# Convolutional attention block on one core: pairs 0 and 1 normalised each by itself, statistics of four pairs on ScalarE, pair 0's bias added behind its products

## The chip, the core and the metric

One NeuronCore of a Trainium2 chip runs the kernel alone. The metric is the device time of one execution in microseconds (us). All times are us unless marked ns. Engines: TensorE (PE), VectorE (DVE), ScalarE (ACT), GpSimd (POOL), and SyncE (SP), which issues transfers.

## What is computed

The input is 16 images of 64 channels and 16 x 16 pixels, all float32. The reference, cut to its core (`_gn` has 32 groups, that is two channels each, and so has the first `group_norm`; the second has one group):

```python
h = _gn(x)
xn = group_norm(h, gn1_w, gn1_b, 32)
qkv = einsum('oc,bchw->bohw', qkv_w, xn) + qkv_b
q, k, v = split(qkv, 3)               # 8 heads of 16, n = 256 pixels
q_norm = softmax(q * scale, axis=-1)  # over pixels
k_norm = softmax(k, axis=-2)          # over the 16 of a head
context = einsum('bhdn,bhen->bhde', k_norm, v)
out = einsum('bhde,bhdn->bhen', context, q_norm)
out = einsum('oc,bchw->bohw', out_w, out) + out_b
out = group_norm(out, gn2_w, gn2_b, 1)
return x + out + h
```

## The kernel before

Two images, a "pair", fill the 128 partitions (2 x 64 channels), so there are 8 pairs, 0 to 7. x is loaded by SyncE in four transfers: pair 0, pair 1, pairs 2 and 3, (then the weights), pairs 4 to 7. The two normalisations of x are folded into one affine, `xn = coef_a * x + coef_b`, per channel and pair.

The program is written out engine by engine; each engine runs its instructions in program order, and semaphores tie the engines together. Nothing is scheduled by a tool: the order around the change is the order of the calls at the end of each engine's block.

The start, per group of pairs (`GROUPED`: pairs 0-1, 2-3, 4-7): VectorE takes `bn_stats` (`raw_stats`, L579) and `bn_aggr` (`channel_moments`, L585) of each pair; TensorE averages over the two channels of a group (`group_average`, L403); VectorE makes the group's variance (`group_variance`, seven small instructions from `dev` to `scaled_mean`, L592 to L610); GpSimd takes the power −1/2 (L217, L231); VectorE makes the coefficients (`group_coefficients`, L617 to L622), and `xn` (L638, pairs 0 and 1; ScalarE makes the later ones, L309). `prepare_bias` (L656) splits the biases into two parts for the matmuls.

Then, for each pair p: TensorE writes the bias (`bias`, L418) and adds the products for keys and values (`keys_values`, L430) in one of two PSUM banks `kv_ps`. VectorE takes the maximum over each head (`key_max`, L677) and subtracts it (`key_shift`, L685); ScalarE takes the exponential (L317); GpSimd sums it by a tree of four additions (L241 to L254); VectorE takes the reciprocal (`key_norm`, L702) and scales the values (`scale_values`, `vs`, L717). TensorE multiplies them to the context (L471), VectorE masks it to its heads (`mask_context`, `ctxm`, L736), TensorE folds the output weights in (`folds`, L485) and ScalarE copies that with the query sums' reciprocal (`fold_copy`, L340). Queries take L446 and L449 on TensorE, their maximum L694 on VectorE, and the exponential L327 on ScalarE. Then TensorE makes the outputs (L508), ScalarE squares and centres them (L351, L359), TensorE averages the squares (L523), VectorE adds eps (`ve`, L760), GpSimd takes the power (`gn2_scale`, `orstd`, L263), VectorE scales it (L768) and makes `res` (`finish`, L778) out of the centred output and `skip`, which GpSimd makes of x (`residual`, L270). SyncE stores each pair.

These stages are pipelined over the pairs: iteration i of the loop (i = 2 to 6) takes the keys of pair i, the values of pair i−1, the outputs of pair i−2 and the result of pair i−3. A tail follows for the last pairs.

TensorE also runs warm-up products (`warm_up`, L395) of ones, whose result nobody reads, into banks that are free at that time; `WARM` holds how many stand at each place.

Of the kernel before, what the change touches and what calls it, by code (L numbers as in the profile page):

```python
# [12 lines left out]
PIX = SIDE * SIDE  # L13
# [12 lines left out]
GROUPED = ((0, 2), (2, 4), (4, 8))  # L26
# [16 lines left out]
WARM = (8, 4, 3, 4, 5, 6, 1)  # L43


def attention_kernel(nc, x, params, weights, b_qkv, matrices, out):
    ctx = ExitStack()
    with ctx:
# [24 lines left out]
        xmv = sb("xmv", [P, PAIRS, 2])  # L73
        dev = sb("dev", [P, PAIRS])
# [27 lines left out]
        ctxm = sb("ctxm", [HIDDEN, 2, TILE])  # L102
# [21 lines left out]
        gavg_banks = (o_ps[0], o_ps[1], o_ps[1])  # L124
# [7 lines left out]
        xstat_ready, xmv_ready, gavg_done = sem("xstat_ready"), sem("xmv_ready"), sem("gavg_done")  # L132
        dev_ready, dev2_ready, gvar_ready = sem("dev_ready"), sem("dev2_ready"), sem("gvar_ready")
# [75 lines left out]
        def _(pool):  # L209
# [4 lines left out]
            def first_rstd():  # L214
                a, b = GROUPED[0]
                pool.wait_ge(pow_ready, 1)
                nc.gpsimd.tensor_tensor(rstd[:, 1, a:b], pow_in[:, 1, a:b], minus_half[:, a:b],  # L217
                                        ALU.pow).then_inc(rstd_ready, 1)

            def first_residual_rstd():  # L220
                a, b = GROUPED[0]
                pool.wait_ge(pow0_ready, 1)
                nc.gpsimd.tensor_tensor(rstd[:, 0, a:b], pow_in[:, 0, a:b], minus_half[:, a:b],
                                        ALU.pow).then_inc(rstd0_ready, 1)
# [11 lines left out]
            def first_key_sums(p):  # L236
# [5 lines left out]

            def key_sums(p):
                r = p % 2
# [29 lines left out]
            first_rstd()  # L274
            group_rstd(1)
            first_residual_rstd()
            for p in range(3):
                first_key_sums(p)
                key_sums(p)
            group_rstd(2)  # L280
            for i in range(3, PAIRS - 1):
                gn2_scale(i - 3)
                first_key_sums(i)
                residual(i - 3)
                key_sums(i)
            gn2_scale(PAIRS - 4)
            for p in range(PAIRS - 4, PAIRS):
# [5 lines left out]
        def _(act):  # L293
# [68 lines left out]
            bias_high()  # L362
            key_exp(0)
            query_exp(0)
            affine(2)
            key_exp(1)
            affine(3)
            query_exp(1)
            for i in range(2, PAIRS - 1):
                fold_copy(i - 2)  # L370
                key_exp(i)
                if i == 3:
                    affine(4)
                if i > 2:
                    affine(i + 2)
# [3 lines left out]
            key_exp(PAIRS - 1)  # L379
            query_exp(PAIRS - 1)  # L380
            fold_copy(PAIRS - 3)
            squares(PAIRS - 3)
            fold_copy(PAIRS - 2)
            fold_copy(PAIRS - 1)
            centred(PAIRS - 3)
# [6 lines left out]
        def _(pe):  # L392
# [5 lines left out]
            def group_average(g):  # L398
                a, b = GROUPED[g]
                pe.wait_ge(xmv_ready, g + 1)  # L400
                if g == 2:
                    pe.wait_ge(pow_ready, 2)
                ins = nc.tensor.matmul(gavg_banks[g][:, AVG:AVG + 2 * (b - a)], avg_group,  # L403
                                       xmv[:, a:b, :], start=True, stop=True, skip_group_check=True)
                if g == 2:
# [6 lines left out]

            def bias(p):
# [3 lines left out]
                for image in range(2):  # L417
                    nc.tensor.matmul(kv_ps[r][:, image, :, :, :, :], ones[rows(image), :],  # L418
                                     bsplit[rows(image), KV].unsqueeze(1).broadcast_to(
                                         [CHANNELS, CHUNKS, 2 * HIDDEN]),  # L420
                                     start=True, stop=False, skip_group_check=True)

            def keys_values(p):
# [4 lines left out]
                for chunk in range(CHUNKS):  # L428
                    for image in range(2):
                        ins = nc.tensor.matmul(kv_ps[r][:, image, chunk, :, :, :],  # L430
                                               xn[rows(image), r, chunk * 128:(chunk + 1) * 128],
                                               w_f[rows(image), KV], start=False, stop=(chunk == CHUNKS - 1),
                                               skip_group_check=True)
                        if chunk == CHUNKS - 1:
# [455 lines left out]
```

## Time and profile before

| | us |
|---|---|
| median of three runs | 56.52 |
| the three runs | 56.21, 56.52, 59.24 |
| the profiled execution | 56.09 |
| its span (first to last instruction) | 54.3 |
| TensorE, VectorE busy in the span | 44.1, 42.0 |
| ScalarE, GpSimd busy in the span | 28.3, 25.6 |
| granted TensorE clock, mean share of full speed | 0.976 |

The span is counted from the first instruction's start to the last one's end; the profiled execution took 1.8 longer than its span. In a timeline row the first number is the start within the span, the second the duration (of the whole row where several instructions are merged, xcount). In square brackets stands how long the engine sat idle before it, and what ended that. The next instruction of an engine can begin before the row of the last one ends, since their ends overlap.

### The profile page before, as it was taken

Reading aid. Unit: us, or ns where it says so; the run is one execution under the profiler, and the core shown is the slowest. Engines: PE = TensorE matmul, PEld = TensorE weight load, DVE = VectorE, ACT = ScalarE, POOL = GpSimd, SP = SyncE. Lnnn points to the kernel's source line nnn. Section 1 sums busy time; section 2 is a strip of 40 time slices with the busy share of each in tenths; the row PEclk is TensorE's granted clock in tenths of the full one; section 3 lists DMA queues with packets and bytes.
Section 4 is the critical chain, followed back from the end, with each engine's and each line's share of the span. In section 5 each row is a group of like instructions: output and inputs, shape, how many; then the busy total and the mean of one; then the engine's idle time right before and its main releaser. Section 6 shows DMA issues by size and latency. Waiting matters only on the chain.

```text
span 54.3 us, 1401 instructions
## 1 busy us (share of the span) xinstructions
PE 44.1 (81%) x439; PEld 29.5 (54%) x439; DVE 42.0 (77%) x145; ACT 28.3 (52%) x88; POOL 25.6 (47%) x55
## 2 busy tenths in 40 slices
PE   2998779994999999599599979979997979895200
PEld 2775258743667665456475764656665754762200
DVE  0048996999999999899999599599686799355640
ACT  0713000079660523994797949677393480768500
POOL 5000404848660068957827916944877920040700
PEclk9999999999999999999999999999999999999955
DMA  0698950000000000000020020011003000002222
GB/s 0 152 280 285 334 206 1 0 0 0 0 0 0 18 0 0 0 0 0 0 97 12 6 97 0 0 43 54 6 0 103 6 6 0 0 0 97 97 97 97
DMA packets 2823, 2.84 MB, mean 52 GB/s; under 512 B 256, under 2 KB 2816, under 8 KB 2816
## 3 DMA queue, kind: packets, MB, share of 16 engines
q1 hardware_dynamic: 2528, 2.49, 14.1%
q10 hardware_dynamic: 288, 0.27, 1.5%
q8 instruction: 3, 0.05, 0.4%
q14 instruction: 4, 0.03, 0.2%
HBM read 1.71 MB, written 1.05 MB: 51 GB/s over the span
## 4 chain that ended last, share of the span: by engine, by line
DVE 32%; PE 31%; issue 13%; ACT 7%; POOL 6%; DMA 5%; ACTq 1%; DVEq 1%; POOLq 0%
PE kv_ps L430 7%; DMA brow<-b_qkv_dram 5%; PE o_ps L485 5%; DVE kmx L677 4%; PE q_ps L449 3%; DVE xstat L579 3%; POOL tree L241 3%; DVE vs L717 3%; PE o_ps L508 3%; DVE ek L685 3%; DVE rks L702 2%; DVE res L778 2%; DVE nqmax L694 2%; PE q_ps L446 2%; DVE ctxm L736 2%
## 5 line engine op out<-in xcount | busy, mean ns | idle before, releaser
L263 POOL TENSOR_TENSOR orstd<-ve,minus_half 128x1 f32<-128x1 f32 x8 | 4.4, 552 | 9.9 <-DVE ve L760 9.9
L317 ACT ACTIVATE ek<-ek 128x512 f32<-128x512 f32 x8 | 5.0, 627 | 7.1 <-DVE ek L685 7.1
L327 ACT ACTIVATE eq<-q_ps,nqmax 128x256 f32<-128x256 f32 x16 | 7.4, 473 | 1.9 <-DVE nqmax L694 1.9
L430 PE MATMUL kv_ps<-w_all,xn 64*128 64x256 f32 x64 | 8.3, 378 | 0.0
L241 POOL TENSOR_TENSOR tree<-ek 128x256 f32<-128x256 f32 x7 | 5.1, 730 | 6.7 <-ACT ek L317 6.7
L395 PE MATMUL kv_ps<-ones 128*128 128x512 f32 x16 | 6.0, 515 | 1.0 <-POOL ones L210 1.0
L430 PEld LDWEIGHTS kv_ps<-w_all,xn 64*128 64x128 f32 x64 | 6.0, 186 | 1.1 <-issue 0.4
L351 ACT ACTIVATE osq<-o_ps,nb 128x256 f32<-128x256 f32 x7 | 3.3, 473 | 6.3 <-DVE nb L751 3.2
L694 DVE TENSOR_REDUCE nqmax<-q_ps 128x2 f32<-128x512 f32 x8 | 5.4, 681 | 0.7 <-PE q_ps L449 0.7
L778 DVE SCALAR_TENSOR_TENSOR res<-oc,coef_o,skip 128x256 f32<-128x256 f32 x8 | 4.4, 548 | 2.0 <-issue 1.9
L717 DVE TENSOR_TENSOR vs<-kv_ps,rks 128x512 f32<-128x512 f32 x8 | 5.5, 692 | 0.3
L579 DVE BATCH_NORM_STATS2 xstat<-x_sb 128x6 f32<-128x256 f32 x8 | 3.1, 418 | 3.4 <-DMA x_sb<-x_dram 3.4
L677 DVE TENSOR_REDUCE kmx<-kv_ps 128x32 f32<-128x512 f32 x8 | 5.4, 676 | 0.4 <-PE kv_ps L430 0.4
L340 ACT ACTIVATE fold<-o_ps,rq 128x65 f32<-128x65 f32 x14 | 3.6, 312 | 3.8 <-PE o_ps L485 3.7
L685 DVE TENSOR_TENSOR ek<-kv_ps,kmx 128x512 f32<-128x512 f32 x8 | 5.4, 679 | 0.1
L471 PEld LDWEIGHTS o_ps<-ek,vs 128*64 128x64 f32 x112 | 3.8, 137 | 2.7 <-issue 2.0
L471 PE MATMUL o_ps<-ek,vs 128*64 128x64 f32 x112 | 4.8, 228 | 0.3 <-DVE vs L717 0.3
L395 PEld LDWEIGHTS kv_ps<-ones 128*128 128x128 f32 x16 | 3.8, 256 | 2.0 <-POOL ones L210 1.0
L449 PE MATMUL q_ps<-xn,w_all 64*128 64x256 f32 x32 | 4.8, 375 | 0.0
L270 POOL TENSOR_SCALAR skip<-x_sb,coef_p,rest 128x256 f32<-128x256 f32 x8 | 4.4, 557 | 0.4 <-DVE rest L632 0.4
L508 PE MATMUL o_ps<-eq,fold 128*64 128x256 f32 x28 | 4.4, 394 | 0.0
L395 PE MATMUL o_ps<-ones 128*128 128x512 f32 x15 | 4.3, 416 | 0.0
(83 smaller groups left out, 84.3 us busy)
## 6 DMA issues: line engine op xcount, KB each, us to landing
out_dram<-res SPq DMA_DIRECT2D x8, 128.0 KB, 1.7
x_sb<-x_dram SPq DMA_DIRECT2D x1, 512.0 KB, 5.5
x_sb<-x_dram SPq DMA_DIRECT2D x2, 128.0 KB, 2.6
x_sb<-x_dram SPq DMA_DIRECT2D x1, 256.0 KB, 4.3
w_all<-weights_dram SPq DMA_DIRECT2D x1, 224.0 KB, 4.7
brow<-b_qkv_dram ACTq DMA_DIRECT2D x1, 192.0 KB, 3.0
mats<-matrices_dram SPq DMA_DIRECT2D x1, 160.0 KB, 5.5
par_avg<-params_dram ACTq DMA_DIRECT2D x1, 67.0 KB, 2.7
```

The lines of the kernel that those rows point to most:

```text
L241: nc.gpsimd.tensor_tensor(tree[:], e[:, :, 0:8], e[:, :, 8:16], ALU.add).then_inc(tree_step, 1)
L327: last = nc.scalar.activation(eq[:, p % 3, image, :], q_ps[:, image, 0, :], ACT.Exp, bias=nqmax[:, r, image:image + 1], accum_out=qs[:, p ...
L395: nc.tensor.matmul(to, ones[:], ones[:].unsqueeze(1).broadcast_to([P, 4, 128]), start=True, stop=True, skip_group_check=True)
L430: ins = nc.tensor.matmul(kv_ps[r][:, image, chunk, :, :, :], xn[rows(image), r, chunk * 128:(chunk + 1) * 128], w_f[rows(image), KV], star ...
L449: nc.tensor.matmul(q_ps[:, image, 0, :], w_f[rows(image), Q], xn[rows(image), r, :], start=False, stop=True, skip_group_check=True).then_i ...
L471: ins = nc.tensor.matmul(context_of(p)[part, image, :], vs[:, r, cols], ek[:, r, cols], start=(image == 0 and chunk == 0), stop=(chunk == ...
L508: ins = nc.tensor.matmul(o_of(p)[rows(image), 0:PIX], fold[:, r, image, 0:CHANNELS], eq[:, p % 3, image, :], start=True, stop=True, skip_g ...
L677: nc.vector.tensor_reduce(kmx[:], half_of(p, 0), AX.X, ALU.max).then_inc(kmax_ready, 1)
L685: nc.vector.tensor_tensor(per_head(ek[:, r, :]), half_of(p, 0), spread(kmx[:]), ALU.subtract).then_inc(ksub_ready, 1)
L694: nc.vector.tensor_reduce(nqmax[:, p % 2, :], q_ps[:, :, 0, :], AX.X, ALU.max, negate=True).then_inc(qmax_ready, 1)
L717: nc.vector.tensor_tensor(per_head(vs[:, r, :]), half_of(p, 1), spread(rks[:]), ALU.mult).then_inc(vs_ready, 1)
L778: nc.vector.scalar_tensor_tensor(out=res[:, p, :], in0=oc[:, r, :], scalar=of(coef_o, r), in1=skip[:, p, :], op0=ALU.mult, op1=ALU.add).th ...
```

## The change

- `GROUPED` gets a group for each of pairs 0 and 1. On VectorE the statistics of pair 0, its aggregate, those of pair 1, and both variance blocks come first; a group of one pair takes one instruction less in `group_variance` and in `group_coefficients`. `prepare_bias` moves behind pair 0's `xn`. `query_max(0)` moves behind the keys of pair 1 and group 2's variance.
- ScalarE measures pairs 2, 3, 6 and 7: a sum by a copy with accumulator, the mean, the sum of squared differences, the variance (`raw_sums`, `raw_squares`). VectorE keeps the statistics of pairs 0, 1, 4 and 5. Group 3's variance and the output bias stand ahead of the loop, its coefficients and the residual's in iteration 2.
- Pair 0's products of keys and values start the PSUM bank, and the bias is added behind them.
- GpSimd: `residual(i−3)` stands ahead of `gn2_scale(i−3)` and of the key sums of iteration i; before, `skip` stood between the first and the second addition of the tree.
- `ctxm` has two buffers. `WARM` is (7, 6, 3, 5, 2, 4) for (8, 4, 3, 4, 5, 6, 1).
- In the tail, VectorE takes `rks` and `vs` of pair 6 ahead of pair 7's query maximum, and `minus_mean(5)` ahead of the last `vs`; ScalarE takes `fold_copy(5)` ahead of the last query exponential and `centred(5)` behind the squares of pair 5.

VectorE, from the keys of pair 0 on, before (`kv_ps0` and `kv_ps1` are the banks of pairs 0 and 1, `nqmax` is a query maximum, `xstat` the statistics of pair 4):

```order
L677 TENSOR_REDUCE kmx<-kv_ps0 128x32
L685 TENSOR_TENSOR ek<-kv_ps0,kmx 128x512
L617 TENSOR_TENSOR mean_a<-rstd,scaled_mean 128x2
L619 TENSOR_SCALAR coef_a<-rstd,par_avg 128x2
L622 TENSOR_SCALAR coef_b<-mean_a,par_avg 128x2
L694 TENSOR_REDUCE nqmax<-q_ps 128x2
L677 TENSOR_REDUCE kmx<-kv_ps1 128x32
L685 TENSOR_TENSOR ek<-kv_ps1,kmx 128x512
L579 BN_STATS xstat<-x_sb 128x6
L702 RECIPROCAL rks<-ks 128x32
L717 TENSOR_TENSOR vs<-kv_ps0,rks 128x512
L694 TENSOR_REDUCE nqmax<-q_ps 128x2
```

and now, from the shift of pair 1's keys on:

```order
L729 TENSOR_TENSOR ek<-kv_ps1,kmx 128x512
L625 TENSOR_TENSOR dev<-xmv,o_ps0 128x2
L627 TENSOR_SCALAR minus_mean_x<-o_ps0 128x2
L634 TENSOR_TENSOR dev2<-dev 128x2
L637 TENSOR_TENSOR gvar<-dev2,o_ps0 128x2
L641 TENSOR_SCALAR pow_in<-gvar 128x2
L644 TENSOR_SCALAR pow_in<-gvar 128x2
L647 TENSOR_SCALAR scaled_mean<-minus_mean_x,par_avg 128x2
L738 TENSOR_REDUCE nqmax<-q_ps 128x2
L611 BN_STATS xstat<-x_sb 128x6
L615 BN_AGGR xmv<-xstat 128x2 x2
L746 RECIPROCAL rks<-ks 128x32
```

The query maximum of pair 0 stood between the keys of pairs 0 and 1; now it stands behind both and behind a variance block.

ScalarE from `bhigh` (the first part of the biases) to the second query exponential, before:

```order
L300 ACTIVATE bhigh<-brow 128x384
L317 ACTIVATE ek<-ek 128x512
L327 ACTIVATE eq,qs<-q_ps,nqmax 128x256 x2
L309 ACTIVATE xn<-x_sb,coef_b,coef_a 128x256
L317 ACTIVATE ek<-ek 128x512
L309 ACTIVATE xn<-x_sb,coef_b,coef_a 128x256
L327 ACTIVATE eq,qs<-q_ps,nqmax 128x256 x2
```

and now (`osq` and `oc` take results that nobody reads, `xsum` the accumulated sums), from pair 0's key exponential on:

```order
L341 ACTIVATE ek<-ek 128x512
L310 ACTIVATE osq,xsum<-x_sb 128x256 x2
L313 ACTIVATE xmv<-xsum 128x2
L341 ACTIVATE ek<-ek 128x512
L351 ACTIVATE eq,qs<-q_ps,nqmax 128x256 x2
L320 ACTIVATE oc,xsum<-x_sb,xmv 128x256 x2
L323 ACTIVATE xmv<-xsum 128x2
L333 ACTIVATE xn<-x_sb,coef_b,coef_a 128x256
L351 ACTIVATE eq,qs<-q_ps,nqmax 128x256 x2
```

The sums of pairs 6 and 7 stand between the two key exponentials, their squares between the query exponential of pair 0 and the `xn` of pair 2.

GpSimd, one round of the loop, before:

```order
L263 TENSOR_TENSOR orstd<-ve,minus_half 128x1
L241 TENSOR_TENSOR tree<-ek 128x256
L270 TENSOR_SCALAR skip<-x_sb,coef_p,rest0 128x256
L246 TENSOR_TENSOR tree2<-tree 128x128
L250 TENSOR_TENSOR tree3<-tree2 128x64
L254 TENSOR_TENSOR ks<-tree3 128x32
```

and now:

```order
L272 TENSOR_SCALAR skip<-x_sb,coef_p,rest0 128x256
L265 TENSOR_TENSOR orstd<-ve,minus_half 128x1
L246 TENSOR_TENSOR tree<-ek 128x256
L248 TENSOR_TENSOR tree2<-tree 128x128
L252 TENSOR_TENSOR tree3<-tree2 128x64
L256 TENSOR_TENSOR ks<-tree3 128x32
```

`skip` moved from behind the first addition to ahead of the power.

The diff, cut to its core:

```diff
...
-GROUPED = ((0, 2), (2, 4), (4, 8))
+GROUPED = ((0, 1), (1, 2), (2, 4), (4, 8))
...
+SUMMED = ((2, 4), (6, 8))
+
+WARM = (7, 6, 3, 5, 2, 4)
...
             pool.wait_ge(half_ready, 1)
-            first_rstd()
-            group_rstd(1)
+            first_rstd(0)
+            first_rstd(1)
+            key_sums(0)
+            first_rstd(2)
+            key_sums(1)
             first_residual_rstd()
-            for p in range(3):
-                first_key_sums(p)
-                key_sums(p)
-            group_rstd(2)
+            group_rstd(3)
+            key_sums(2)
             for i in range(3, PAIRS - 1):
+                residual(i - 3)
                 gn2_scale(i - 3)
-                first_key_sums(i)
-                residual(i - 3)
                 key_sums(i)
...
+            def raw_sums(n):
+                a, b = SUMMED[n]
+                act.wait_ge(x_in[load_of(a)], DMA)
+                for p in range(a, b):
+                    nc.scalar.activation(osq[:, p % 2, :], x_sb[:, p, :], ACT.Copy,
+                                         accum_out=xsum[:, 0, p:p + 1]).then_inc(xsum_ready, 1)
+                act.wait_ge(xsum_ready, 2 * n + 2)
+                nc.scalar.activation(xmv[:, a:b, 0], xsum[:, 0, a:b], ACT.Copy,
+                                     scale=1.0 / PIX).then_inc(xmean_ready, 1)
+
+            def raw_squares(n):
+                a, b = SUMMED[n]
+                act.wait_ge(xmean_ready, n + 1)
+                for p in range(a, b):
+                    nc.scalar.activation(oc[:, p % 2, :], x_sb[:, p, :], ACT.Square, bias=xmv[:, p, 0:1],
+                                         scale=-1.0, accum_out=xsum[:, 1, p:p + 1]).then_inc(xsq_ready, 1)
+                act.wait_ge(xsq_ready, 2 * n + 2)
+                nc.scalar.activation(xmv[:, a:b, 1], xsum[:, 1, a:b], ACT.Copy,
+                                     scale=1.0 / PIX).then_inc(xvar_ready, 1)
...
             bias_high()
+            raw_sums(0)
+            raw_squares(0)
             key_exp(0)
+            raw_sums(1)
+            key_exp(1)
             query_exp(0)
+            raw_squares(1)
             affine(2)
-            key_exp(1)
+            query_exp(1)
             affine(3)
-            query_exp(1)
...
             def group_average(g):
                 a, b = GROUPED[g]
-                pe.wait_ge(xmv_ready, g + 1)
-                if g == 2:
-                    pe.wait_ge(pow_ready, 2)
+                if g != 2:
+                    pe.wait_ge(xmv_ready, min(g, 2) + 1)
+                if g >= 2:
+                    pe.wait_ge(xvar_ready, g - 1)
+                    pe.wait_ge(pow_ready, g - 1)
...
             warm_up(WARM[0], early)
             pe.wait_ge(par_in, DMA)
             group_average(0)
+            group_average(1)
             warm_up(WARM[1], early)
-            bias(0)
-            group_average(1)
-            warm_up(WARM[2], early)
             pe.wait_ge(w_in, DMA)
             keys_values(0)
+            bias(0)
+            group_average(2)
             bias(1)
             keys_values(1)
             queries(0)
+            pe.wait_ge(pow_ready, 2)
+            warm_up(WARM[2], o_ps[1][:])
+            queries(1)
+            group_average(3)
+            pe.wait_ge(pow_ready, 3)
             warm_up(WARM[3], o_ps[0][:])
-            queries(1)
-            warm_up(WARM[4], o_ps[0][:])
             bias(2)
             keys_values(2)
             context(0)
-            group_average(2)
...
-            warm_up(WARM[5], o_of(PAIRS - 2))
+            warm_up(WARM[4], o_of(PAIRS - 2))
             context(PAIRS - 2)
             means(PAIRS - 3)
             outputs(PAIRS - 3)
-            warm_up(WARM[6], kv_ps[0][:, 1, :, :, :, :])
+            warm_up(WARM[5], kv_ps[0][:, 1, :, :, :, :])
...
             group_variance(0)
-            raw_stats(2)
-            raw_stats(3)
-            channel_moments(1)
+            group_variance(1)
             group_coefficients(0)
             affine(0)
+            prepare_bias()
+            group_coefficients(1)
             affine(1)
-            group_variance(1)
             prepare_weights()
             key_max(0)
             key_shift(0)
-            group_coefficients(1)
-            query_max(0)
+            raw_stats(4)
             key_max(1)
             key_shift(1)
-            raw_stats(4)
+            group_variance(2)
+            query_max(0)
+            raw_stats(5)
+            channel_moments(4)
+            channel_moments(5)
             key_norm(0)
             scale_values(0)
+            group_coefficients(2)
+            group_variance(3)
+            output_bias()
             query_max(1)
...
             key_shift(PAIRS - 1)
-            query_max(PAIRS - 1)
             key_norm(PAIRS - 2)
             scale_values(PAIRS - 2)
+            query_max(PAIRS - 1)
             query_norm(PAIRS - 2)
             last_key_sums()
             key_norm(PAIRS - 1)
+            minus_mean(PAIRS - 3)
             scale_values(PAIRS - 1)
             mask_context(PAIRS - 2)
-            minus_mean(PAIRS - 3)
```

## Rows read from the trace of the kernel before

**Rows 1.** Timeline of SyncE's queue, 0 to 10: start, duration, what is issued

```profile
0.72 1.34 SPq L199 DMA_DIRECT2D x_sb<-x_dram  x3
2.10 0.47 SPq L201 DMA_DIRECT2D w_all<-weights_dram  x1
```

**Rows 2.** The page, part 6: transfers, KB each, median us from issue to landing

```profile
x_sb<-x_dram SPq DMA_DIRECT2D x1, 256.0 KB, 4.3
w_all<-weights_dram SPq DMA_DIRECT2D x1, 224.0 KB, 4.7
```

**Rows 3.** The chain that ended last, in order of time: start, us, what

```profile
4.70 0.62 DVE bsplit L656
...
8.28 1.11 PE kv_ps L430 x8
...
9.48 0.70 DVE kmx L677
```

**Rows 4.** Timeline of VectorE, 0 to 27

```profile
5.23 0.15 DVE L592 TENSOR_TENSOR dev<-xmv,o_ps 128x2 f32<-128x2 f32 x1
...
6.08 0.75 DVE L579 BATCH_NORM_STATS2 xstat<-x_sb 128x6 f32<-128x256 f32 x2
...
16.82 0.69 DVE L677 TENSOR_REDUCE kmx<-kv_ps 128x32 f32<-128x512 f32 x1
...
21.11 0.69 DVE L677 TENSOR_REDUCE kmx<-kv_ps 128x32 f32<-128x512 f32 x1
...
26.56 0.66 DVE L677 TENSOR_REDUCE kmx<-kv_ps 128x32 f32<-128x512 f32 x1
```

**Rows 5.** Timeline of ScalarE: the first exponential of queries

```profile
11.86 0.47 ACT L327 ACTIVATE eq<-q_ps,nqmax 128x256 f32<-128x256 f32 x1 [0.30 <-DVE nqmax L694]
```

**Rows 6.** Timeline of TensorE, 0 to 22

```profile
0.97 3.42 PE L395 MATMUL kv_ps<-ones 128*128 128x512 f32 x8 [0.97 <-POOL ones L210]
...
13.68 1.43 PE L395 MATMUL o_ps<-ones 128*128 128x512 f32 x5
15.04 0.50 PE L418 MATMUL kv_ps<-bsplit,ones 64*128 64x512 f32 x2
15.38 1.02 PE L430 MATMUL kv_ps<-w_all,xn 64*128 64x256 f32 x8
...
17.20 0.36 PE L407 MATMUL o_ps<-par_avg,mats 128*128 128x1 f32 x2
```

**Rows 7.** Timeline of GpSimd in the loop, iteration 5

```profile
34.33 0.57 POOL L270 TENSOR_SCALAR skip<-x_sb,coef_p,rest 128x256 f32<-128x256 f32 x1
```

**Rows 8.** Timelines of VectorE and TensorE in the loop, 31 to 40

```profile
31.07 0.67 DVE L677 TENSOR_REDUCE kmx<-kv_ps 128x32 f32<-128x512 f32 x1
...
34.99 0.61 DVE L778 SCALAR_TENSOR_TENSOR res<-oc,coef_o,skip 128x256 f32<-128x256 f32 x1 [0.62 <-issue]
...
40.11 0.66 DVE L677 TENSOR_REDUCE kmx<-kv_ps 128x32 f32<-128x512 f32 x1
...
31.99 0.45 PE L485 MATMUL o_ps<-w_all,ctxm 64*64 64x65 f32 x8 [0.29 <-DVE ctxm L736]
...
34.15 1.03 PE L430 MATMUL kv_ps<-w_all,xn 64*128 64x256 f32 x8
```

**Rows 9.** Timelines of VectorE and TensorE in the tail

```profile
42.36 0.69 DVE L694 TENSOR_REDUCE nqmax<-q_ps 128x2 f32<-128x512 f32 x1 [0.72 <-PE q_ps L449]
...
45.11 0.69 DVE L717 TENSOR_TENSOR vs<-kv_ps,rks 128x512 f32<-128x512 f32 x1
...
51.72 0.48 DVE L778 SCALAR_TENSOR_TENSOR res<-oc,coef_o,skip 128x256 f32<-128x256 f32 x1
...
48.64 0.63 PE L508 MATMUL kv_ps<-eq,fold 128*64 128x256 f32 x4
```

**Rows 10.** Stretches: length, busy (x), and granted clock (PEclk), DMA, GB/s

```profile
51.50:51.75 0.25, 0.00 (x0) 0.00 (x0) 0.21 (x2) 0.00 (x0) 0.00 (x0) 0.80 0.00 0
51.75:52.00 0.25, 0.00 (x0) 0.00 (x0) 0.25 (x1) 0.00 (x0) 0.00 (x0) 0.50 0.00 0
```

More of the change, by code:

```diff
@@ L101, in attention_kernel @@
         rq = sb("rq", [HIDDEN, 2, 2])
-        ctxm = sb("ctxm", [HIDDEN, 2, TILE])
+        ctxm = sb("ctxm", [HIDDEN, 2, 2, TILE])
         fold = sb("fold", [HIDDEN, 2, 2, FOLDS])
@@ L417, in bias @@
                 for image in range(2):
[L418 to L421, printed above, removed]
+                    ins = nc.tensor.matmul(kv_ps[r][:, image, :, :, :, :], ones[rows(image), :],
+                                           bsplit[rows(image), KV].unsqueeze(1).broadcast_to(
+                                               [CHANNELS, CHUNKS, 2 * HIDDEN]),
+                                           start=(p > 0), stop=(p == 0), skip_group_check=True)
+                    if p == 0:
+                        ins.then_inc(kv_done[image], 1)
             def keys_values(p):
@@ L431, in keys_values @@
                                                xn[rows(image), r, chunk * 128:(chunk + 1) * 128],
-                                               w_f[rows(image), KV], start=False, stop=(chunk == CHUNKS - 1),
-                                               skip_group_check=True)
-                        if chunk == CHUNKS - 1:
+                                               w_f[rows(image), KV], start=(p == 0 and chunk == 0),
+                                               stop=(p > 0 and chunk == CHUNKS - 1), skip_group_check=True)
+                        if p > 0 and chunk == CHUNKS - 1:
                             ins.then_inc(kv_done[image], 1)
@@ L484, in folds @@
                         part = slice(t * TILE, (t + 1) * TILE)
-                        nc.tensor.matmul(o_of(p)[part, folded(image)], ctxm[part, image, :], wo_sb[part, :],
+                        nc.tensor.matmul(o_of(p)[part, folded(image)], ctxm[part, p % 2, image, :], wo_sb[part, :],
                                          start=(image == 0), stop=True,
@@ L579, in raw_stats, with channel_moments @@
                 nc.vector.bn_stats(xstat[:, p, :], x_sb[:, p, :]).then_inc(xstat_ready, 1)
-            def channel_moments(g):
-                a, b = GROUPED[g]
-                for p in range(a, b):
-                    dve.wait_ge(xstat_ready, p + 1)
-                    ins = nc.vector.bn_aggr(xmv[:, p, :], xstat[:, p, :])
-                ins.then_inc(xmv_ready, 1)
+            def channel_moments(p):
+                dve.wait_ge(xstat_ready, p + 1 if p < 2 else p - 1)
+                ins = nc.vector.bn_aggr(xmv[:, p, :], xstat[:, p, :])
+                if p != 4:
+                    ins.then_inc(xmv_ready, 1)
             def group_variance(g):
@@ L734, in mask_context @@
                 dve.wait_ge(ctx_done, TILES * (p + 1))
-                wait(dve, fold_done, 2 * TILES * p)
-                nc.vector.tensor_tensor(ctxm[:], context_of(p),
+                wait(dve, fold_done, 2 * TILES * (p - 1))
+                nc.vector.tensor_tensor(ctxm[:, p % 2, :, :], context_of(p),
                                         mats[:, HEAD_MASK].unsqueeze(1).broadcast_to([P, 2, TILE]),
```

92 lines of the change are left out of this document (48 added, 44 removed).

## The prediction

> **What bounds the kernel now.** I read the page first: no engine is busy throughout, and the chain that ended last changes between TensorE and VectorE. So I went on to that chain in order of time, and then to each engine's timeline, to see what each stretch waits for.
>
> The chain's first stretch runs through the biases: `bsplit` at 4.70 stands ahead of the first group's variance, which starts at 5.23; the keys and values of pair 0 run on TensorE from 8.28 and the first key maximum starts at 9.48 [rows 3, 4]. From there VectorE is nearly full up to the key maxima of pairs 2, 3 and 4 (16.82, 21.11, 26.56) [rows 4].
>
> In the steady loop the key maxima are 4.52 apart (31.07 to 40.11 is two periods of it) [rows 8]. In every one VectorE stands still for 0.62 before `res`: it waits for `skip`, which GpSimd makes from 34.33 to 34.90 behind `tree`, and `res` starts at 34.99 [rows 7, 8]. That is a queueing stall on GpSimd, not work.
>
> In the tail VectorE waits 0.72 for the last queries before `nqmax` at 42.36, and `rks`, `vs` of pair 6 are queued behind it; the last `vs` starts at 45.11, the last outputs at 48.64, the last `res` ends at 52.20 [rows 9].
>
> **The change, part by part.** All starts are worked forward from durations of these rows; "K2" is the start of the key maximum of pair 2.
>
> *First pair.* Its statistics no longer wait for pair 1 and its variance not for `bsplit`. A group's variance block takes 0.85 (5.23 to 6.08) [rows 4], for one pair without one dependent step. I put `xn` of pair 0 at about 6.6. But the weights are issued at 2.10 and land 4.7 later, at 6.8 [rows 1, 2]: they end last now. Keys and values then run 6.85 to 7.85; the bias pair follows them (0.34, as 15.04 to 15.38 [rows 6]). Before, start of the products to key maximum was 1.20 [rows 3]; now 1.20 + 0.43 for two biases and their drain. **K0 = 8.5, a gain of 1.0.**
>
> *ScalarE's statistics.* Four 256-column sums and four squares, with an accumulator, and four small scalings are new. The nearest row is the exponential with accumulator (that at 11.86 is 0.47 long) [rows 5]. No row shows a source in SBUF with an accumulator; bounds are 0.35 and 0.6 each; I take 0.47. Two with a 0.2 scaling and a semaphore make 1.2. Pairs 2 and 3 land at 1.6 + 4.3 = 5.9 (third of three issues from 0.72 to 2.06) [rows 1, 2], so their variance is there at 8.4, TensorE waits 0.3 for it ahead of pair 1's bias, and K1 = 10.2. What it takes off VectorE is four statistics passes at 0.33 (two in 0.66, 6.08 on) and four aggregates, about 1.7 [rows 4].
>
> *Where that goes.* Behind K1: shift at 10.95, then group 2's variance block 11.55 to 12.4, and only then pair 0's query maximum. It stood ahead of K1 before. So ScalarE's exponentials of pair 0's queries run 13.1 to 14.05 instead of from 11.86 [rows 5], and behind them come the squares of pairs 6 and 7 (14.05 to 15.3). Group 3's average on TensorE needs these: 15.35. It and the output bias product take 0.6 to the result (the second alone is 0.36 long at 17.20, and starts about 0.25 behind the first) [rows 6]. VectorE reaches group 3's variance at 15.0 and waits for it until 16.0: **a new wait of 1.0**, with query maximum 1 and everything behind it queued. On TensorE five warm-up products (1.36, from 13.68 to 15.04) now stand between that average and pair 2's bias and products (0.34 and 1.1) [rows 6]: 15.85, 17.2, 17.55, 18.5. VectorE would be ready at 18.0. **K2 = 18.6 against 16.82: 1.8 lost.** Affine 2 is ready at about 15.95, so it is the warm-ups that end last there.
>
> *Iterations 2 and 3.* In the first of them a variance block and the output bias leave VectorE, and group 3's coefficients and the residual's, as many small instructions, come in: the period stays 4.3 (16.82 to 21.11 [rows 4]), K3 = 22.9. In the next, which took 5.45 before (21.11 to 26.56), those six small instructions are gone from VectorE (0.9 to 1.1); TensorE takes over as the bound: pair 0's output mean is subtracted at 22.7; ScalarE squares and centres it until 23.8 and then takes the query exponentials of pair 2 until 24.65; TensorE makes the variance at 24.0, folds 1 at 24.3, queries 3 behind those exponentials at 24.8, outputs 1 at 25.7, bias 4 at 26.2 and its products from 26.6 to 27.55. So K4 = 27.6 against 26.56: of the 1.8, 0.8 has been given back.
>
> *The steady loop.* On GpSimd `skip` is now made ahead of `orstd` and `tree`, in time that GpSimd idles, so the 0.62 ahead of `res` goes [rows 7, 8]. What is late next is TensorE: folds at 31.99 are 0.92 behind the key maximum at 31.07, and the products end at 35.2 [rows 8], which is 3.24 behind the folds. So a period is 0.92 + 3.24 + 0.1 = 4.26, not 4.52 − 0.62 = 3.90. Three periods end with such a stall: 3 × 0.26 = 0.8 gained. K7 = 40.4 against 40.11. The second `ctxm` buffer costs and gives nothing, since the folds that the mask waited for are by then over 3 old.
>
> *The tail.* `rks` and `vs` of pair 6 run in the 0.72 [rows 9] where VectorE waited for the queries. Behind K7 this gives: `rks` 1.5, `vs` 1.85, query maximum 2.45 (queries are there at 2.2), last key sums 3.1, `rks` 3.8, and the last `vs` 4.2 instead of 5.0. TensorE: context 6 at 2.6, outputs 5 at 3.35, four warm-ups (0.27 each) until 5.0, just when `vs` is done, context 7 at 5.0, folds 6 at 5.6, variance 5 at 6.0, folds 7 at 6.3 (mask 7 ends at 6.0), outputs 6 at 6.8, outputs 7 at 7.5 instead of 8.53: **1.0 gained**, and all behind it is the same chain (nb, squares, variance, root, scale, `res`).
>
> *Sum.* Last `res` ends at 52.20 + 0.3 − 1.0 = 51.5; that is −0.7. The profiled execution took 56.09, so 55.4; the median of the three runs is 56.52, and one of them is 59.24, so I compare with about 56.3.
>
> **The clock.** TensorE gets a gap: three warm-ups end at 11.75, and queries 1 wait for the exponentials until 14.3. Then 0.75 of work, 0.3 of waiting, and the dense part starts at 15.85. In the kernel before no gap is longer than 0.8 before the end. There the granted clock is 0.80 from 51.50 to 51.75 and 0.50 behind it [rows 10], that is 1.2 instead of 2.4 GHz; the engine's last long stretch of work ended at 49.3, with two 0.4 pieces behind it. So it fell some 2.3 behind the dense work. The new gap is as long as that.
>
> The Trainium skill (TensorE: Matmul & The Clock Gate, "What's actually happening") has the lower level as the default that only recent activity lifts, and where in a gap it falls differs by run; this case's end agrees (0.50 from 51.75). By that rule the time would come out as the first rival's.
>
> **Rivals.**
>
> 1. *The clock falls in the new gap.* For it: the row at the end. Against it: 0.75 of work stands in the middle of the gap. Price: a warm-up at the low level is 0.43 apart (eight in 3.42, at the start) against 0.27 [rows 6]. For the length of the low stretch I take that of the start as an estimate, 3.4. The dense part from 15.85 would be low to about 19.3: warm-ups end at 18.1, bias at 18.7, products at 20.0. That is 1.5 more, **56.9**; if it recovers by 17.7, 0.7 more, 56.1.
>
> 2. *Slower than before by the same place.* The clock stays low through the products and context of pair 2: products take 2.1, K2 = 20.7, 2.2 more, **57.6**. It decides from the point where the low level lasts beyond 20. Against it: the low stretch at the start was shorter than that.
>
> 3. *The stall ahead of `res` moves instead of going.* `skip` ahead of `orstd` could hold the latter. `orstd` waits for `ve` 1.5 behind the key maximum and `skip` is done before it in my working; but if the period stays 4.52, the 0.8 goes and the time is **56.2**.
>
> 4. *More is gained.* If the squares of pairs 6 and 7 cost 0.35 each, and VectorE, not the warm-ups, sets K2, 0.6 more comes; with a tail gain of 1.4 rather than 1.0 (the last folds without any warm-up in the way) it is **54.4**.
>
> **How the numbers follow.** Forecast case (55.4, own range 54.8 to 55.9): 0.55. Rival 1: 0.17. Rival 2: 0.05. Rival 3: 0.08. Rival 4: 0.15. The range of 8 in 10 goes from 54.3 to 56.9: it leaves out rival 2 and the edges of 1 and 4. A measurement of this kernel can tell about 2% from no change, which is 55.2 against 56.3; under it lie all of rival 4 and a good part of the forecast case. Faster by over 2%: 0.41. Within: 0.43. Slower: 0.16, from rivals 1 and 2 and an error of the start's sum.
>
> **What would show it.** Right: first `kmx` near 8.5; a VectorE wait of about 1 for the group average near 15 to 16; third `kmx` at 18 to 19; `res` without idle time ahead of it in the loop, and periods near 4.26; the last `vs` 4.2 behind the last `kmx`; clock 1.00 up to 51. Wrong: third `kmx` at 17 or earlier (the wait does not exist and the time is under 54.5), or a granted clock of 0.5 anywhere between 13 and 20 (rivals 1 and 2), or periods still at 4.5 (rival 3).

## The result and the profile after

The changed kernel takes 59.09 us (median of four runs, 58.86 to 60.05). Against the kernel before it is slower: the ratio is 1.047, with a 95% interval of 1.036 to 1.058. Some executions of either kernel take 1 to 3 us longer than its others (59.24 and 59.15 of four before, 60.05 of four after); the ratio leaves those out. Its profiled execution took 58.93, with a span of 57.1, against 56.09 and 54.3.

| start of the key maximum, or end | before | forecast | after |
|---|---|---|---|
| K0 (pair 0) | 9.48 | 8.5 | 8.65 |
| K2 | 16.82 | 18.6 | 21.60 |
| K3 | 21.11 | 22.9 | 26.14 |
| K4 | 26.56 | 27.6 | 31.08 |
| K7 | 40.11 | 40.4 | 43.87 |
| last `res` ends | 52.20 | 51.5 | 55.02 |
| execution | 56.09 | 55.4 | 58.93 |

From K0 to K2 it now takes 5.6 longer (12.95 for 7.34). K0 comes 0.8 earlier and the way from K2 to the last `res` is 2.0 shorter (33.4 for 35.4), which leaves a loss of 2.8. The page after, part 2 (busy tenths of TensorE and its clock in 40 slices), shows what is new there. One digit is a slice of 1.43; PEclk is the granted clock in tenths of full speed.

```profile
PE   3998598930799996994899899899899899997200
PEclk9999999999555569999999999999999999999975
```

Stretches of that time (length, busy time and count of PE, PEld, DVE, ACT, POOL, then the granted clock, DMA share, GB/s):

```profile
12.00:13.00 1.00, 0.00 (x0) 0.00 (x0) 0.93 (x8) 0.63 (x1) 0.84 (x4) 1.00 0.00 0
13.00:14.00 1.00, 0.00 (x0) 0.00 (x0) 1.00 (x5) 0.43 (x2) 1.00 (x2) 1.00 0.00 0
14.00:14.25 0.25, 0.00 (x0) 0.00 (x0) 0.25 (x2) 0.25 (x3) 0.17 (x2) 0.85 0.00 0
14.25:14.50 0.25, 0.00 (x0) 0.00 (x0) 0.22 (x2) 0.25 (x3) 0.25 (x1) 0.50 0.00 0
...
20.75:21.00 0.25, 0.25 (x4) 0.25 (x2) 0.00 (x0) 0.00 (x0) 0.00 (x0) 0.50 0.00 0
21.00:21.25 0.25, 0.25 (x4) 0.06 (x2) 0.00 (x0) 0.00 (x0) 0.00 (x0) 1.00 0.00 0
```

TensorE has nothing to do from 11.9 on. Its clock falls to 1.2 GHz at 14.2, 0.4 before the gap ends, and is back at 2.4 GHz only at 21.0, although TensorE works without a break from 14.64 on. All four executions of the changed kernel have a mean granted clock of 0.923 to 0.930, so this is not the profiled one alone. The timeline of TensorE in that time, to be held against [rows 6] (the five warm-ups were 1.43, bias and products 0.50 and 1.02):

```profile
10.93 0.96 PE L420 MATMUL o_ps<-ones 128*128 128x512 f32 x3
14.64 0.58 PE L476 MATMUL q_ps<-scales,bsplit 64*128 64x256 f32 x2 [2.75 <-ACT eq L351]
15.02 1.05 PE L479 MATMUL q_ps<-xn,w_all 64*128 64x256 f32 x4
16.00 0.59 PE L430 MATMUL o_ps<-xmv,par_avg 128*128 128x8 f32 x2
16.45 0.56 PE L434 MATMUL o_ps<-par_avg,mats 128*128 128x1 f32 x2
16.88 2.48 PE L420 MATMUL o_ps<-ones 128*128 128x512 f32 x5
19.29 0.79 PE L446 MATMUL kv_ps<-bsplit,ones 64*128 64x512 f32 x2
19.88 1.58 PE L460 MATMUL kv_ps<-w_all,xn 64*128 64x256 f32 x8
```

The chain that ended last now runs through these (start, us, what); in the kernel before, nearly all of the chain from 14 to 21 was VectorE's:

```profile
17.01 2.34 PE o_ps L420 x5
19.36 0.72 PE kv_ps L446
20.08 1.44 PE kv_ps L460 x7
```

VectorE waits twice for TensorE, for group 3's average and for pair 2's products:

```profile
17.05 0.16 DVE L625 TENSOR_TENSOR dev<-xmv,o_ps 128x4 f32<-128x4 f32 x1 [1.67 <-PE o_ps L434]
...
21.60 0.69 DVE L721 TENSOR_REDUCE kmx<-kv_ps 128x32 f32<-128x512 f32 x1 [2.63 <-PE kv_ps L460]
```

In the loop, `res` starts without idle time ahead of it, the 0.62 of [rows 8] is gone, and the engine is idle for TensorE instead:

```profile
34.31 0.48 DVE L822 SCALAR_TENSOR_TENSOR res<-oc,coef_o,skip 128x256 f32<-128x256 f32 x1
...
35.34 0.69 DVE L721 TENSOR_REDUCE kmx<-kv_ps 128x32 f32<-128x512 f32 x1 [0.48 <-PE kv_ps L460]
...
39.61 0.69 DVE L721 TENSOR_REDUCE kmx<-kv_ps 128x32 f32<-128x512 f32 x1 [0.48 <-PE kv_ps L460]
```

### The profile page after: what moved, and what is told of

The parts are those of the page before. It is cut to its first block, busy times and chain, and to the rows that moved or that the text cites. A ratio compares the mean times of both kernels' runs of the same rounds, so it can differ in the third digit from the quotient of the medians.

```text
span 57.1 us, 1419 instructions
## 1 busy us (share of the span) xinstructions
PE 45.9 (80%) x437; PEld 30.8 (54%) x437; DVE 41.3 (72%) x143; ACT 33.2 (58%) x108; POOL 26.6 (47%) x56
## 3 DMA queue, kind: packets, MB, share of 16 engines
HBM read 1.71 MB, written 1.05 MB: 48 GB/s over the span
## 4 chain that ended last, share of the span: by engine, by line
PE 57%; DVE 12%; ACT 10%; DMA 8%; issue 7%; SPq 1%; DVEq 0%; ACTq 0%
PE kv_ps L460 12%; DMA x_sb<-x_dram 8%; PE q_ps L479 6%; PE kv_ps L446 6%; PE o_ps L420 5%; PE o_ps L538 5%; PE o_ps L515 5%; PE o_ps L501 5%; PE q_ps L476 4%; ACT eq L351 3%; DVE ctxm L780 3%; DVE kmx L721 2%; DVE res L822 2%; PE kv_ps L420 2%; PE o_ps L526 2%
## 5 line engine op out<-in xcount | busy, mean ns | idle before, releaser
L460 PE MATMUL kv_ps<-w_all,xn 64*128 64x256 f32 x64 | 8.9, 399 | 0.6 <-DMA w_all<-weights_dram 0.6
L460 PEld LDWEIGHTS kv_ps<-w_all,xn 64*128 64x128 f32 x64 | 6.6, 204 | 2.0 <-DMA w_all<-weights_dram 1.1
L476 PE MATMUL q_ps<-scales,bsplit 64*128 64x256 f32 x16 | 3.4, 418 | 2.8 <-ACT eq L351 2.8
L446 PE MATMUL kv_ps<-bsplit,ones 64*128 64x512 f32 x16 | 4.4, 544 | 0.0
L333 ACT ACTIVATE xn<-x_sb,coef_b,coef_a 128x256 f32<-128x256 f32 x6 | 3.6, 597 | 1.1 <-DVE coef_b L666 0.9
```

Source lines behind the costliest of these rows:

```text
L446: ins = nc.tensor.matmul(kv_ps[r][:, image, :, :, :, :], ones[rows(image), :], bsplit[rows(image), KV].unsqueeze(1).broadcast_to([CHANNELS ...
L460: ins = nc.tensor.matmul(kv_ps[r][:, image, chunk, :, :, :], xn[rows(image), r, chunk * 128:(chunk + 1) * 128], w_f[rows(image), KV], star ...
L476: nc.tensor.matmul(q_ps[:, image, 0, :], bsplit[rows(image), Q], scales[rows(image), 0:PIX], start=True, stop=False, skip_group_check=True)
```

## Two theories and the experiments

The clock theory says that the new gap lets the clock fall, and the low clock makes the loss. The order theory says that the new waits (query exponentials, squares and group average, all later) make it slow whatever the clock does. "K0 to K2" below is from the start of pair 0's key maximum to that of pair 2; it takes out most of what comes from a late first key maximum, which differs between executions of one kernel. It is 7.34 before and 12.95 after.

### The gap filled

```diff
-WARM = (7, 6, 3, 5, 2, 4)
+WARM = (7, 6, 13, 5, 2, 4)
```

> The changed kernel with 13 instead of 3 warm-up products ahead of queries 1, so that TensorE works until those queries can start. Clock theory (the granted clock fell to 0.50 from 14.2 to 21.0 because of the gap from 11.75 to 14.6, and that is what made the kernel slower): the granted clock stays 1.00, the warm-ups end at 14.5 and hold nothing up, the key maximum of pair 2 starts at 18.9 instead of 21.6, and the profiled time is 58.9 - 2.7 = 56.2. Order theory (the new waits, for the query exponentials and for the group average, make it slower whatever the clock): the key maximum of pair 2 stays above 20.5 and the time above 58.

Measured: ratio to the kernel before 0.9996 (0.9954 to 1.0038), seven of ten executions between 55.98 and 56.60, none over 57.96; the changed kernel had none under 58.86. The profiled one took 57.84 and not the expected 56.2, because its K0 is at 10.29, 1.64 later than in the changed kernel (its first groups ran at half the pace, see the last section); without that it is 56.2. K0 to K2 is 10.26, 2.7 less. Of this, 0.3 may come from the late K0 itself, since K0 to K1 is 1.66 here and 1.93 in the changed kernel; from K1 to K2 it is 8.60 for 11.02, 2.4 less. Its page:

```profile
PE   3997999999966996993999999899899899996200
PEclk9999999999999999999999999999999999999975
```

The five warm-ups take 1.39 from 17.72, not 2.48, and VectorE's waits are 1.05 and 0.73 for 1.67 and 2.63:

```profile
17.89 0.16 DVE L625 TENSOR_TENSOR dev<-xmv,o_ps 128x4 f32<-128x4 f32 x1 [1.05 <-PE o_ps L434]
...
20.55 0.69 DVE L721 TENSOR_REDUCE kmx<-kv_ps 128x32 f32<-128x512 f32 x1 [0.73 <-PE kv_ps L460]
```

More work on TensorE, none of it needed, gave back the whole slowdown. The order theory falls as the cause of the slower time. But there is no gain left either: with the clock kept, the change is worth nothing. K0 to K2 is still 2.9 longer than the 7.34 before; that part is the order's.

### The five warm-ups behind queries 1 taken out

```diff
-WARM = (7, 6, 3, 5, 2, 4)
+WARM = (7, 6, 3, 0, 2, 4)
```

> The changed kernel without the five warm-up products ahead of pair 2's bias, the gap ahead of queries 1 left as it is. They ran from 16.88 to 19.29 at the low clock. If they are what ended last there (clock theory's account of the path), bias 2 starts at 16.9, the key maximum of pair 2 at about 19.2, 2.4 earlier, and the time is 56.5, with the clock still at 0.50 from 14.2 on. If another wait stands behind them (the affine of pair 2, the query maximum of pair 1), less than 1 is gained: over 57.9. If the clock stays low longer because TensorE does less, the loop's first periods get longer than 4.9 and part of the gain goes again.

Measured: ratio 1.061 (1.052 to 1.070), three executions at 59.44 to 59.48 and the profiled one at 60.26: no better than the changed kernel (1.047, 1.036 to 1.058). Most of the 2.4 expected to K2 is there: K0 to K2 is 10.67, 2.3 less than after, and K1 to K2 is 9.00 for 11.02, 2.0 less. It is all lost in what follows: K2 to K4 takes 11.96, where it took 9.48. The page shows why:

```profile
PEclk9999999999755555555599999999999999999975
```

The clock was low from 15.3 to 29.0, 13.7, instead of for 6.8. The products of a pair's keys and values were nearly twice as long for pairs 2 and 3 (1.91 for 1.02):

```profile
25.71 1.91 PE L460 MATMUL kv_ps<-w_all,xn 64*128 64x256 f32 x8
```

So the warm-ups were on the path and cost 2.0 to 2.3 there. In the three traces that keep the five and have the fall ahead of them (this change, and two experiments below), the clock is back after 6.8; without the five it took 13.7. That they bought the clock's earlier return is the reading that fits; what it is about them that does so was not tested.

### The kernel before with a wider gap

```diff
-WARM = (8, 4, 3, 4, 5, 6, 1)
+WARM = (8, 4, 3, 0, 5, 6, 1)
```

> The kernel before without its four warm-up products ahead of queries 1: its gap there grows from 0.8 to 2.0, nothing else moves. Clock theory: if a gap of 2.0 is enough, the granted clock falls to 0.50 at about 13 to 14 and the time goes up by 1.5 to 3, to 58 to 59; if it is not, the time stays within 0.3 of the kernel before and the limit lies between 2.0 and the 2.75 of the change. Order theory: no change at all, since those products end 0.8 before the queries can start.

Measured: ratio 1.0005 (0.9986 to 1.0024); five of ten executions at 56.31 to 56.36, the others from 57.5 to 60.7 (of the kernel before, beside it, four of 19 took over 57). The profiled one keeps the clock over the gap, and K0 to K2 is 7.32:

```profile
12.96 0.39 PE L446 MATMUL q_ps<-scales,bsplit 64*128 64x256 f32 x2 [1.95 <-ACT eq L327]
```

A gap of 1.95 between dense stretches need not bring the clock down. None of the long executions has a trace. The mean clock of the two at 60.7 is 0.959, that of the five at 56.3 is 0.960 to 0.983, four of them within 0.961, so the record does not show a fall there; of those at 57.5 to 57.8 two have 0.931 and 0.935, so the clock may have fallen in them, and where is open.

### Pair 0's query maximum earlier

```diff
-            group_variance(2)
-            query_max(0)
+            query_max(0)
+            group_variance(2)
```

> The changed kernel with pair 0's query maximum ahead of group 2's variance block (0.85 long) instead of behind it. Queries 1 and the squares of pairs 6 and 7 come 0.85 earlier, the gap on TensorE shrinks from 2.75 to 1.9. Clock theory: if the clock then stays at 1.00, the key maximum of pair 2 starts at 18.1 and the time is 55.4; if it still falls, only 0.85 is gained, 58.1. Order theory: 0.85 gained, 58.1, in either case.

Measured: 59.04 to 60.03 in three executions, 56.90 in one. In the profiled one K0 to K2 is 12.06, 0.89 less, so the 0.85 is real. The gap is 1.80, and the clock still fell, at 15.1, and again at 28.7, that time with TensorE at work:

```profile
PEclk9999999999655559999855999999999999999975
```

```profile
13.69 0.39 PE L476 MATMUL q_ps<-scales,bsplit 64*128 64x256 f32 x2 [1.80 <-ACT eq L351]
```

The length of the one gap does not decide: the clock fell here with 1.80 and stayed up with the 1.95 above. Ahead of 15.1 stood the gap, 0.8 of queries, and a wait of 0.44. The execution of 56.90 is 1.5 above the 55.4 expected for a kept clock, and its mean clock is 0.947, where executions with the gap filled have 0.971 to 0.982; so it probably had a fall too, and none of the four shows the clock kept.

### The gap halved

```diff
-WARM = (7, 6, 3, 5, 2, 4)
+WARM = (7, 6, 8, 5, 2, 4)
```

> The changed kernel with 8 instead of 3 warm-ups ahead of queries 1: the gap there shrinks from 2.75 to 1.4. Clock theory with a graded chance: with the gap at 2.75 every execution took 58.9 or more, filled none took over 58.0. Here the clock stays at 1.00 in most executions and these take 56.2, as with the gap filled; the others 58.5 or more. Order theory: 58 or more in all.

Measured: 61.13, 58.42, 57.70 and 56.79. The last three had a mean clock of 0.974 to 0.983, as the executions with the gap filled (0.971 to 0.982). The first had 0.933, and in its trace the gap is 1.61, the clock is low from 17.3 to 24.1, 6.8, and K0 to K2 is 12.90:

```profile
16.26 0.39 PE L476 MATMUL q_ps<-scales,bsplit 64*128 64x256 f32 x2 [1.61 <-ACT eq L351]
```

Its K0 is also late, at 10.52, which is why it is longer than the changed kernel. By their mean clock three of four kept the clock, which fits the graded chance of the expectation, but only one of them is near 56.2; why the others took 57.70 and 58.42 is open without a trace. Four executions are few for a chance.

### Only the loop's new order

The kernel before with GpSimd's order changed from iteration 4 on:

```diff
             for i in range(3, PAIRS - 1):
+                if i > 3:
+                    residual(i - 3)
                 gn2_scale(i - 3)
                 first_key_sums(i)
-                residual(i - 3)
+                if i == 3:
+                    residual(i - 3)
                 key_sums(i)
+            residual(PAIRS - 4)
             gn2_scale(PAIRS - 4)
-            for p in range(PAIRS - 4, PAIRS):
+            for p in range(PAIRS - 3, PAIRS):
                 residual(p)
```

> The kernel before with only the new order of GpSimd in the loop from iteration 4 on: skip ahead of orstd and the tree. Queueing theory (the idle 0.62 ahead of res is the wait for skip, and TensorE is late next): res starts without idle time ahead of it, the period is 4.26 to 4.27 instead of 4.52 in the three iterations that had the stall, 0.8 less in all, 55.3 where the kernel before takes 56.1. Rival (another wait of the loop, such as the key sums behind orstd, was as long): the period stays above 4.4 and less than 0.3 is gained.

Measured: ratio 0.9885 (0.9860 to 0.9911), three executions from 55.73 to 55.87 and one of 57.26. The periods are 4.34, 4.26 and 4.27 for 4.51, 4.53 and 4.51, so 0.68 less in the trace (expected 0.8; the first of the three gives 0.17 and not 0.26). The stall is gone, and the next wait is for TensorE, so the rival is out:

```profile
34.22 0.48 DVE L782 SCALAR_TENSOR_TENSOR res<-oc,coef_o,skip 128x256 f32<-128x256 f32 x1
...
35.25 0.69 DVE L681 TENSOR_REDUCE kmx<-kv_ps 128x32 f32<-128x512 f32 x1 [0.47 <-PE kv_ps L434]
```

### Only the new tail

```diff
-            query_max(PAIRS - 1)
             key_norm(PAIRS - 2)
             scale_values(PAIRS - 2)
+            query_max(PAIRS - 1)
...
+            minus_mean(PAIRS - 3)
             scale_values(PAIRS - 1)
             mask_context(PAIRS - 2)
-            minus_mean(PAIRS - 3)
...
+            fold_copy(PAIRS - 3)
             query_exp(PAIRS - 1)
-            fold_copy(PAIRS - 3)
             squares(PAIRS - 3)
+            centred(PAIRS - 3)
...
-WARM = (8, 4, 3, 4, 5, 6, 1)
+WARM = (8, 4, 3, 4, 5, 2, 4)
```

> The kernel before with only the new tail: rks and vs of pair 6 ahead of the last query maximum, minus_mean 5 ahead of the last vs, fold_copy 5 and centred 5 moved on ScalarE, and 2 and 4 warm-ups for 6 and 1. The last vs starts 4.2 to 4.3 behind the last key maximum instead of 5.0, and the last res ends 11.1 behind it instead of 12.1: 1.0 less, 55.1. Rival (the end is bound by ScalarE's copies and squares, which do the same work): under 0.4 less, 55.7 or more.

Measured: ratio 0.9884 (0.9849 to 0.9919), which rests on two executions, 55.72 and 55.86; the other two took 58.28 and 59.27. In the trace (of 58.28, with K0 at 12.38) the last `vs` starts 4.19 behind K7 and the last `res` ends 11.35 behind it, where it was 12.09: 0.74 less, three quarters of the expected 1.0.

The missing 0.2 is there in the changed kernel (11.15). What differs is its second `ctxm` buffer, which this kernel lacks: with one buffer the mask of pair 7 waits for the folds of pair 6, with two for its own context. The first row is from the next experiment, which has this tail too and K7 at 39.54, the second from the changed kernel, K7 at 43.87; the mask starts 6.24 and 5.79 behind K7. No run changes the buffer alone.

```profile
45.78 0.29 DVE L740 TENSOR_TENSOR ctxm<-kv_ps,mats 128x128 f32<-128x128 f32 x1 [1.01 <-PE o_ps L489]
...
49.66 0.29 DVE L780 TENSOR_TENSOR ctxm<-kv_ps,mats 128x128 f32<-128x128 f32 x1 [0.57 <-PE kv_ps L501]
```

### Loop and tail together, with the old start

The two diffs above in one kernel.

> The kernel before with both the new GpSimd order in the loop and the new tail, and the old start. If the parts add up, 0.8 + 1.0 = 1.8 less, 54.3. If they share a gain, 55 or more. This also says what the new start costs: the changed kernel with the gap filled has all three parts and took as long as the kernel before, so the start would cost 1.8.

Measured: **ratio 0.972 (0.967 to 0.977)**, four executions from 54.69 to 55.17. Within the intervals the parts add up: 0.65 and 0.65 alone, 1.6 together, about 0.2 short of the expected 1.8. This kernel beats both. The changed kernel with the gap filled has the same loop order and tail order, the second `ctxm` buffer as well, and took as long as the kernel before. So the new start, with iterations 2 and 3 as they come with it, costs about 1.6 with the clock kept.

```profile
39.54 0.69 DVE L681 TENSOR_REDUCE kmx<-kv_ps 128x32 f32<-128x512 f32 x1 [0.47 <-PE kv_ps L434]
...
43.81 0.69 DVE L721 TENSOR_TENSOR vs<-kv_ps,rks 128x512 f32<-128x512 f32 x1
...
50.44 0.48 DVE L782 SCALAR_TENSOR_TENSOR res<-oc,coef_o,skip 128x256 f32<-128x256 f32 x1
```

### What the new start loses besides the clock

```diff
-WARM = (7, 6, 3, 5, 2, 4)
+WARM = (7, 6, 10, 0, 2, 4)
...
             key_exp(1)
+            raw_squares(1)
             query_exp(0)
-            raw_squares(1)
...
-            queries(1)
             group_average(3)
+            queries(1)
```

> The changed kernel with the squares of pairs 6 and 7 ahead of pair 0's query exponentials on ScalarE, group 3's average ahead of queries 1 on TensorE, 10 warm-ups ahead of it to fill the gap and none behind queries 1. If the late squares, the wait for the group average and the five warm-ups are what the new start loses (order theory for the rest), VectorE does not wait for group 3's average, the key maximum of pair 2 starts 8.6 behind that of pair 0 instead of 10.3 (gap filled) or 12.95 (changed kernel), and the time is 54.5. If something else behind them is as late (the affine of pair 2 behind the exponentials), it starts 9.5 or more behind and the time is over 55.4.

Measured: K0 to K2 is 8.52 (expected 8.6), and VectorE goes from one block to the next without the wait for the average:

```profile
14.74 0.22 DVE L666 TENSOR_SCALAR coef_b<-mean_a,par_avg 128x2 f32<-128x2 f32 x1
14.87 0.14 DVE L625 TENSOR_TENSOR dev<-xmv,o_ps 128x4 f32<-128x4 f32 x1
```

So the late squares, the average behind queries 1 and the five warm-ups, taken away together, were the new start's loss apart from the clock: K2 is at 16.91, as the 16.82 before. Which of the three was worth how much was not measured. The executions are 54.91, 55.80, 56.08 and 56.52. The first, whose mean clock was 0.992, is as expected. In the profiled one (55.80) the clock fell elsewhere, in iteration 3, and K3 to K4 took 6.50 instead of 4.94:

```profile
24.00:24.50 0.50, 0.50 (x10) 0.31 (x8) 0.40 (x3) 0.47 (x1) 0.00 (x0) 0.89 0.00 0
24.50:25.00 0.50, 0.50 (x4) 0.07 (x2) 0.50 (x1) 0.27 (x1) 0.45 (x1) 0.50 0.00 0
```

TensorE had idled for 0.49 at 17.4 and for 0.94 at 21.7. With the gap filled it idled for as long at the same two places (0.49 ahead of 21.51, 0.94 ahead of 26.25) and the clock stayed at 1.00, so these waits alone are not the cause, which stays open. The best of the four, 54.91, is within the range of the old start with the same loop and tail order (54.69 to 55.17), the other three are above it: this start is no better than the old one.

### The best kernel with its own gap filled

```diff
-WARM = (8, 4, 3, 4, 5, 2, 4)
+WARM = (8, 4, 3, 7, 5, 2, 4)
```

> The kernel before with the new loop order and the new tail, and 7 instead of 4 warm-ups ahead of queries 1, which fill the gap of 0.8 there. The loop and the tail are worth 1.6 as measured: 54.8. The three further warm-ups (0.8) just fit, so they cost nothing; if they hold up queries 1, up to 0.1 is lost. They can only change how often the clock falls, not the time of an execution in which it stays.

Measured: ratio 0.975 (0.971 to 0.979), five executions from 54.67 to 55.18 and one of 58.06. The three extra warm-ups cost nothing that can be measured and did not keep away the one long execution. That one's trace says why: there the clock was low at the start, not in the gap (below).

## Why the prediction was wrong, step by step

**The first pair.** K0 at 8.65 for 8.5. The weights landed 5.0 behind their issue instead of 4.7, and the products started at 7.15 instead of 6.85; from there to K0 it took 1.50, where 1.63 was taken. Right.

**ScalarE's statistics.** The sums are 0.42 apart and the squares 0.51, where 0.47 was taken. The variance of pairs 2 and 3 was there at 8.7, K1 at 10.58 for 10.2. The late landing is most of it. Right.

**Where that goes.** Query exponentials from 13.57 (forecast 13.1), the squares until 15.6 (15.3), the average at 16.00 (15.35), VectorE at its variance block at 15.4 and waiting until 17.05:

```profile
13.57 0.47 ACT L351 ACTIVATE eq<-q_ps,nqmax 128x256 f32<-128x256 f32 x1 [0.91 <-DVE nqmax L738]
```

Gap and waits are as worked; the gap was 2.75 for 2.55. At the low clock queries 1 last until 16.0, later than the squares and their scaling (15.8), so it was those products that the average came behind. With the gap filled K0 to K2 measures 10.26, and the forecast's is 10.1. This part was right, and so was the reading that warm-ups end last there.

**The step that failed is the clock.** The prediction put the new gap beside the end of the trace before, noted that it was as long as the stretch after which the clock had fallen there, and still gave the fall 0.22 in all (rivals 1 and 2) because 0.75 of work stood in the middle. The clock fell at 14.2, before that work began, so the work could not guard it. Filling the gap took the fall away and 2.4 to 2.7 of the way to K2 with it, which is the evidence that the fall made the slowdown. The stretch read at the end of the trace was not a fixed length either: in the trace of the kernel before with the wider gap, with the same last products, the dense work ended at 49.3 and the clock fell at 50.2, 0.9 behind it, not 2.3. The price was also too small. The low stretch of the start, 3.4, was taken as the estimate and counted from 15.85; it lasted 6.8 from 14.2. So what came true is the mechanism of rival 2, which was given 0.05: the five warm-ups took until 19.3, the products until 21.4, K2 = 21.6, where rival 2 said 20.7. Its time, 57.6, is nearest to the 58.93 measured, and still 1.3 short. The rule of the Trainium skill cited there (TensorE: Matmul & The Clock Gate, "What's actually happening"), by which the low level is the default that only recent activity lifts, agrees with this trace: 0.50 from 14.25. It does not settle the case by itself: in the runs the clock fell after a gap of 1.80 and stayed up over one of 1.95.

**Iterations 2 and 3.** K2 to K3 is 4.54 for 4.3: the block that came in is not as short as the one that left. Coefficients of group 3 and of the residual take from 24.01 to 25.41, 1.4; variance block and output bias took 1.15. K3 to K4 is 4.94 for 4.7, with the clock kept too (4.93 with the gap filled). These two terms, 0.5, were sized too small.

**The loop.** Periods 4.26, 4.27 and 4.26 for 4.26. Right, and so was what is late next, TensorE.

**The tail.** The last `vs` 4.26 behind K7 (4.2) and the last `res` ending 11.15 behind it (11.1). The 1.0 is right (0.94). But the prediction says of the second `ctxm` buffer that it "costs and gives nothing", while its 1.0 has mask 7 done at 6.0; the tail without that buffer brought 0.74, so 0.2 of the 1.0 goes with it.

**The sum.** Without the fall the steps give 8.65 + 10.26 + 4.53 + 4.93 + 12.79 + 11.14 = 52.3 for the end of the last `res`, where the forecast had 51.5 and the kernel before 52.2. The 10.26 is from a trace with a late K0; with the changed kernel's K0 to K1 it would be 10.5, and the end 52.6. So the forecast's gain of 0.7 was not there either: 0.5 is lost in iterations 2 and 3, 0.3 to 0.6 at the start. With the clock kept the change would have measured as no change, which the gap filled shows (0.9996).

## What to carry to other kernels

A reordering on other engines that gives TensorE a longer gap has to be charged with what the clock does there, before anything else, and for the dense stretch behind the gap too: here the fall in a gap of 2.75 cost about 2.7, on top of the 1.6 that the new start costs with the clock kept. Work a change out stretch by stretch and measure its parts alone: two of this one's three parts were worth 1.6 together, and the third lost it even with the clock kept. Warm-up products are not free where they stand on the path, but taking them out can cost as much further on.

## What the runs showed of the hardware

The low clock can outlast the start's low stretch, with TensorE busy almost throughout: it lasted 6.8 after the gap of 2.75 and also after those of 1.80 and 1.61, and 13.7 where the five warm-ups were left out, with one wait of 0.49 in it. Where it fell with TensorE at work (24.4 with the squares first, 28.7 with the query maximum earlier), it lasted 3.4. In the first of these the waits of more than 0.4 in the 7 before the fall were 0.49 and 0.94.

How long the low clock of the start lasts differs between executions of kernels that start alike. In the best kernel with its gap filled, the execution of 58.06 ran its first groups at half speed to about 13, so K0 was at 12.64 instead of the 9.61 of the same kernel without the filling. The late K0 makes nearly the whole of its 3.1 over the others. The traced executions of 57.84 (gap filled, K0 at 10.29) and 58.28 (tail only, K0 at 12.38) are long for the same reason. Timeline of TensorE in that of 58.06 (in [rows 3] the products took 1.11 on the path):

```profile
5.71 2.05 PE L399 MATMUL kv_ps<-ones 128*128 128x512 f32 x4
...
10.42 2.08 PE L434 MATMUL kv_ps<-w_all,xn 64*128 64x256 f32 x8
```

The record of the granted clock does not show this. It reads 1.00 from the start of every trace here, also where products of 512 columns are 0.43 apart, as the first eight of [rows 6] in their 3.42, and not 0.27 as later. Until the first change in the record, the products' own pace is what tells the clock.
